# Mixture-of-experts tiles of 256 rows, with one small tile of 128 rows for each expert's odd block

## The reference, cut to what matters

```python
logits = xt @ Wr + br                       # 6250 x 8
top_p, top_idx = top_k(softmax(logits), 2)
weights = top_p / top_p.sum(-1)
xn = layernorm(xt)
xe = xn * ln_g[e] + ln_b[e]                 # per expert e
h = gelu(xe @ W1[e] + b1[e])                # 256 -> 1024
y = h @ W2[e] + b2[e]                       # 1024 -> 256
out = sum over the two chosen e of weights * y
```

## Time and profile before

| | us |
|---|---|
| median of 3 runs | 1971.73 (1967.81 to 1977.33) |
| the profiled execution | 1971.06 |
| its span on the core | 1969.4 |
| PE / DVE / ACT / POOL busy in the span | 1594.7 / 1144.1 / 884.5 / 1136.7 |

### The profile page before, as it was taken

One profiled execution on the slowest core, in us unless ns is written; L12 is line 12 of the kernel. 1 busy time (PEld: TensorE's weight loads), 2 busy tenths in 40 slices (PEclk: granted clock), 3 DMA queues, 4 the chain that ended last, 5 costly groups with the idle time before them and its releaser, 6 DMA issues. The chain is left out here.

```text
span 1969.4 us, 32441 instructions
## 1 busy us (share of the span) xinstructions
PE 1594.7 (81%) x8582; PEld 1313.8 (67%) x8583; DVE 1144.1 (58%) x3175; ACT 884.5 (45%) x1872; POOL 1136.7 (58%) x1141
## 2 busy tenths in 40 slices
PE   6766667767777787887777836789999999999997
PEld 5645455555655554555555635679999999999996
DVE  6622222322345466675765679767777777777774
ACT  6611111111213233343443456556666666666664
POOL 3177777777777677777777627753333333333333
PEclk9988888888888899998888955689999999999999
DMA  8344444344346667666677557598778887877875
GB/s 217 116 128 127 110 121 121 115 119 119 112 137 227 203 191 223 205 209 206 211 225 222 144 183 259 175 301 233 222 219 216 217 220 223 219 215 214 217 222 127
DMA packets 188121, 368.81 MB, mean 187 GB/s; under 512 B 33324, under 2 KB 134172, under 8 KB 173656
## 3 DMA queue, kind: packets, MB, share of 16 engines
q0 software_dynamic: 77296, 252.50, 45.5%
q1 hardware_dynamic: 102992, 113.64, 18.2%
q10 hardware_dynamic: 7736, 1.52, 0.4%
HBM read 287.94 MB, written 80.39 MB: 187 GB/s over the span
## 5 line engine op out<-in xcount | busy, mean ns | idle before, releaser
L697 POOL DMA_INDIRECT w2s_lent<-z_d,edge_tabs_lent x784 | 774.4, 988 | 293.0 <-issue 247.0
L1309 DVE TENSOR_TENSOR acc_lent<-acc_lent,bank 128x258 f32 x244 | 102.5, 420 | 473.9 <-PE bank L1818 470.5
L1818 PE MATMUL bank<-w2s_lent,G 128*128 x976 | 282.2, 441 | 110.5 <-POOLq L685 110.5
L1818 PE MATMUL bank<-w2s_lent,S_lent 128*128 x976 | 267.9, 424 | 84.2 <-POOLq L685 81.9
L2028 PE MATMUL bank<-w2s 128*128 128x512 f32 x896 | 330.6, 403 | 5.8 <-DMA w2s<-w_d 5.8
L1818 PEld LDWEIGHTS bank<-w2s_lent,G 128*128 128x128 f32 x976 | 208.6, 220 | 177.6 <-issue 141.5
L741 POOL DMA_INDIRECT out_dram<-G,acc_lent x112 | 178.7, 1596 | 211.0 <-DVE G L1652 162.5
L1818 PEld LDWEIGHTS bank<-w2s_lent,S_lent 128*128 128x128 f32 x976 | 200.1, 211 | 148.7 <-issue 115.1
L1033 ACT ACTIVATE G<-bank,acc_lent 128x256 f32<-128x256 f32 x448 | 187.9, 471 | 193.8 <-PE bank L2009 107.8
L2007 PE MATMUL bank<-w2s,acc 128*128 128x256 f32 x896 | 258.4, 288 | 3.5 <-DVE w2s L1631 3.0
L2008 PE MATMUL bank<-w2s,acc 128*128 128x256 f32 x896 | 253.3, 283 | 0.0
(11 more groups left out here) (316 smaller groups left out, 2562.8 us busy)
## 6 DMA issues: line engine op xcount, KB each, us to landing
w2s<-w_d POOLq DMA_DIRECT2D x112, 1024.0 KB, 5.7
w_d<-w2s_lent SPq DMA_DIRECT2D x64, 256.0 KB, 3.6
acc_lent<-bucket_d SPq DMA_DIRECT2D x56, 266.0 KB, 2.9
w2s_lent<-z_d,edge_tabs_lent POOLq DMA_INDIRECT x784, 2.9
bu_d<-w2s_lent SPq DMA_DIRECT2D x98, 128.0 KB, 1.8
w2s_lent<-bu_d SPq DMA_DIRECT2D x14, 768.0 KB, 8.0
w1s<-in_L_ffn_W_dram SPq DMA_DIRECT2D x8, 1024.0 KB, 6.1
w2s_lent<-in_L_ffn_W_dram SPq DMA_DIRECT2D x32, 256.0 KB, 5.2
```

The lines of the kernel that those rows point to most:

```text
L697: pool.indirect_dma_start(out=ring_rows[:, row % (RING * QUAD), 0:D], out_offset=None, in_=z_d[:, :], in_offset=bass.IndirectOffsetOnAxis( ...
L1309: dve.tensor_tensor(to, to, bank[j % DEPTH][:, 0:ACCW], ALU.add).then_inc(s["acc_done"], 1)
L1818: m = pe.matmul(bank[j % DEPTH][:, 0:ACCW], S_of[j % DEPTH][:, k, :], rows[:, ds(bases[j], ACCW)], start=(k == 0), stop=(k == QUAD - 1))
```

## The change

The number of tiles goes from 56 of 256 rows to 49 of 256 (`BIG`) and eight small ones of 128, 57 in all. `last_tiles` gives each expert floor(blocks / 2) big tiles and one small tile if its count of 128-row blocks is odd; small tiles that are left over take halves of further tiles of 256. The small tiles stand at fixed places in the order: 8, 15, 22, 29, 36, 43, 50 and the last, 56. The loop is gone: all 57 turns are written out on every engine, and waits that were computed from the loop's register are constants.

In a small tile the high and the low part of the turned rows lie side by side, in one operand of 256 columns. `layer1` then has two products where there were three: high weights x (high | low) with 256 columns, and low weights x high with 128 columns, 8 products in a quarter. The two halves of the sum stand in different columns of PSUM, so VectorE adds them (`add_terms`, new), and the Gelu reads `raw` in place of PSUM. The rest is halved in rows: transposes, `hhi`, `hlo`, `weigh`, scatter, and `layer2`, which has 2 pairs of products in a quarter in place of 4. First weights and `layer2`'s weights are loaded and split as for a big tile.

```diff
-MOE_TILES = (2 * N + EXPERTS * (MT - 1)) // MT
+UNITS = (2 * N + EXPERTS * (P - 1)) // P
+BIG = (UNITS - EXPERTS + 1) // 2
+MOE_TILES = BIG + EXPERTS
+SMALL_AT = [8 + 7 * k for k in range(EXPERTS - 1)] + [MOE_TILES - 1]
...
-            repeat(eng, links, two, EARLY // 2 - 1, MOE_TILES // 2 - 1)
-            body(MOE_TILES - 2, 0)
-            body(MOE_TILES - 1, 1)
+        def moe_tiles(eng, body):
+
+            for i in range(2, MOE_TILES):
+                if i == EARLY - 2:
+                    eng.wait_ge(s["moetab_set"], 2)
+                body(i, i % 2)
...
+            def add_terms(t, q):
+
+                dve.wait_ge(s["h_mm"], MOE_PARTS * t + q + 1)
+                until(dve, s["h_hi"], MOE_PARTS * t + q - 1)
+                until(dve, s["h_split"], MOE_PARTS * t + q - 1)
+                two = bank[q % 2][:, :].rearrange("p (k n) -> p k n", n=MT)
+                L.after(dve.tensor_copy(hidden_raw(t, q), two[:, :, P:2 * P]))
+                dve.tensor_tensor(hidden_raw(t, q), two[:, :, 0:P], hidden_raw(t, q), ALU.add).then_inc(s["h_sum"], 1)
...
+                if in_range(i, 1) and small(i + 1):
+                    add_terms(i + 1, 0)
                 for q in range(MOE_PARTS):
                     if in_range(i, 2):
                         first_weights(i + 2, q, e)
                     if in_range(i, 1):
+                        if small(i + 1) and q + 1 < MOE_PARTS:
+                            add_terms(i + 1, q + 1)
                         dve.wait_ge(s["h_hi"], MOE_PARTS * (i + 1) + q + 1)
...
-                        act.wait_ge(s["h_mm"], n + 1)
-                        until(act, s["h_split"], n - 1)
+                        if small(i + 1):
+                            act.wait_ge(s["h_sum"], sums_done(i + 1, q))
+                            frm, w = raw[q % 2], P
+                        else:
+                            act.wait_ge(s["h_mm"], n + 1)
+                            until(act, s["h_split"], n - 1)
+                            frm, w = bank[q % 2], MT
...
+                        if small(t):
+                            x_both = xhi[par][:, k * MT:(k + 1) * MT].bitcast(F32R)
+                            pe.matmul(to, hi, x_both, start=(k == 0), stop=(k == DC - 1), skip_group_check=True)
+                            m = pe.matmul(to[:, 0:P], lo, x_both[:, 0:P], start=False, stop=(k == DC - 1), skip_group_check=True)
+                            continue
```

More of the change, by code:

```diff
@@ L328, in build_program @@
         early_rows = tiny2(2)
+        less_half, at_slot, small_no = (tiny2(1) for _ in range(3))
         small3 = [xTs[:, :], edge_tabs[:, RT * PAYW:2 * P * EJ]]
@@ L397, in build_program, with small, halves, slot_of @@
         out_t = out.rearrange("(t p) d -> p t d", p=P)
[L399 to L406, removed]
-            repeat(eng, links, two, EARLY // 2 - 1, MOE_TILES // 2 - 1)
-            body(MOE_TILES - 2, 0)
-            body(MOE_TILES - 1, 1)
+        def moe_tiles(eng, body):
[3 more added lines that the diff above has]
+                body(i, i % 2)
+        def small(t):
+            return t in SMALL_AT
+        def halves(t):
+            return 1 if small(t) else 2
+        def slot_of(t):
+            if small(t):
+                return SMALL_SLOT + SMALL_AT.index(t)
+            return t - sum(at < t for at in SMALL_AT)
+        def added(t):
+            return 16 * sum(halves(k) for k in range(t))
+        def sums_done(t, q):
+            return MOE_PARTS * SMALL_AT.index(t) + q + 1
         def turns_of_a(t):
@@ L591, in _, with load_xe @@
                     load_ub(g + 2)
-            def load_xe(t, h, turn):
-                r = sp.value_load(moetab[0:1, ds(t, 1)], min_val=0, max_val=PADROW)
+            def load_xe(t):
+                h, n = t % 2, halves(t)
+                r = sp.value_load(moetab[0:1, slot_of(t):slot_of(t) + 1], min_val=0, max_val=PADROW)
                 until(sp, s["xe_free"], t - 1)
[L596 to L600, removed]
+                sp.dma_start(xe[h][:, 0:n, :], bucket_d[ds(r, n * P), :].rearrange("(j p) w -> p j w", p=P)).then_inc(pair["xe_in"][h], 16)
             sp.wait_ge(s["moetab_set"], 1)
@@ L1598, in last_tiles @@
             def last_tiles():
-                rc, ec = ss6[:, 0:1], ss6[:, 1:2]
+                rc, ec, rc_odd, ec_odd, is_odd, at = (ss6[:, k:k + 1] for k in range(6))
                 dve.wait_ge(s["mtab_cnt"], 2)
@@ new lines, in last_tiles @@
+                L.after(dve.tensor_scalar(ci, ci, 7, None, ALU.logical_shift_right))
+                dve.tensor_copy(units, ci)
+                L.after(dve.tensor_scalar(row8.bitcast(I32), ci, 1, None, ALU.logical_shift_right))
+                L.after(dve.tensor_copy(ntf, row8.bitcast(I32)))
+                dve.scalar_tensor_tensor(out=row8, in0=ntf, scalar=float(MT), in1=eoff, op0=ALU.mult, op1=ALU.add)
+                L.after(dve.scalar_tensor_tensor(out=odd, in0=ntf, scalar=-2.0, in1=units, op0=ALU.mult, op1=ALU.add))
@@ L1614, in last_set @@
+                dve.tensor_tensor(rc_odd, rc_odd, rc, ALU.subtract)
+                L.after(dve.tensor_tensor(ec_odd, ec_odd, ec, ALU.subtract))
+                dve.scalar_tensor_tensor(out=tile_table[:, 0:1], in0=rc_odd, scalar=is_odd, in1=rc, op0=ALU.mult, op1=ALU.add)
+                dve.scalar_tensor_tensor(out=tile_table[:, 1:2], in0=ec_odd, scalar=is_odd, in1=ec, op0=ALU.mult, op1=ALU.add
+                                         ).then_inc(s["mtab_ready"], 1)
             def last_set():
@@ L2040, in moe @@
                     if q == 1 and in_range(i, 2):
[L2041 to L2053 removed]
+                        turn_x(i + 2, par, (i + 2) // 2)
             layer1(0, 0, 0)
@@ L2064, in _ @@
             moe(1, 1)
-            for turn in range(1, EARLY // 2 - 1):
-                two(turn)
-            pe.wait_ge(s["moetab_set"], 2)
-            repeat(pe, None, two, EARLY // 2 - 1, MOE_TILES // 2 - 1)
-            moe(MOE_TILES - 2, 0)
-            moe(MOE_TILES - 1, 1)
+            moe_tiles(pe, moe)
 N_WEIGHTS = 20
```

157 lines of the change are left out of this document (89 added, 68 removed).

## The result

| | before | after |
|---|---|---|
| median, us | 1971.63 (1967.81 to 1977.33, 4 runs) | 1981.93 (1977.95 to 1985.81, 4 runs) |
| ratio | | 1.0059 (95% interval 1.0041 to 1.0077) |
| the profiled execution, its span | 1971.06, 1969.4 | 1977.95, 1976.3 |
| expert stage: start of the transposes of tile 3 to the end of the span | 1307.78 to 1969.4: 661.6 | 1304.46 to 1976.3: 671.8 |

The changed kernel is 0.6% slower. The last line of the table leaves out what varies between executions ahead of the experts (in this one the profile of after reached tile 3 earlier by 3.3 us), so the traces are compared by it: **+10.2 us**.

The account below looks back on a forecast made before the run. TensorE was taken to bound the expert stage at 12.04 us a turn. Seven big tiles less (-84.3), seven inner small ones (+84.4) and the last (+8.4) gave +8.5 on 1971.06, 1979.6, forecast as 1980 us; range 1966 to 1998.

Parts of the forecast that it names:

- TensorE alone: TensorE's own work for a small tile, layers 1 and 2, transposes and bias: 6.5 us, bounds 6.0 and 9.8.
- The chain sets the turns: Around a small tile, serial sum, Gelu and first weights on VectorE and ScalarE, 2.83 us a quarter, set two turns.
- turns s-1 and s: Turn s-1 does layer 1 of small tile s, turn s its layer 2; turn s begins at 13.24, s+1 at 24.27.
- Wait before quarter 2: In turn s-1, TensorE idles 2.1 us before quarter 2 of layer 1, needing the hhi of quarter 0.
- Its links: Per quarter: copy and add 0.89 us, two Gelus with handover 0.56, first weights' high part 0.63, handover 0.14, low part 0.61.
- An inner small tile costs 12.05 us: Each of seven small tiles before the last costs as much as a big one; halved matmuls are paid back as waiting.
- removing the branch gives nothing: Writing out the expert loop gains zero, since transposes stand 12.04 us apart also across the loop's end.
- The last tile saves 3.6 us: Tile 56, without successor, has a short VectorE chain and costs 12.04 - 3.6 us; bounds of the saving 2.8 and 5.5.
- Rival 1, the clock: Clock falls in TensorE's new waits around small tiles: +5 to +21 us on top, 1985 to 2000; chance 0.22.
- Rival 2, TensorE the bound: TensorE still sets the turns, sums and Gelus running ahead of first weights: 1936 to 1965, mostly 1939; chance 0.07.
- Rival 3, a lighter chain: Small tiles' chain lighter than its bounds, or last tile and missing loop give more: about 1965 us; chance 0.06.
- Rival 4, fetches: Written-out turns starve for instructions beside weight loads, some 40 more packets for TensorE: 2015 if each costs 1 us; chance 0.05.

Follow-up runs that it names:

- the written-out run: The kernel before, still with 56 tiles of 256 rows, with only the loops over the tiles written out: 1967.93 us, ratio 0.9990 to before.
- the run with the sums ahead: The changed kernel with copy and sum of quarter q+1 put ahead of the first weights' low part of quarter q on VectorE: 1966.82 us, ratio 0.9984 to before.

## Why the prediction was right, and where it wasn't

Forecast 1980 (1966 to 1998), measured 1981.93. The total is close, and partly by luck: two terms of the sum were off, by -2.7 and +4.2 us, and their errors nearly cancel:

| term, us | predicted | measured |
|---|---|---|
| one turn more | 12.04 | 12.04 |
| seven inner small tiles against big ones | +0.1 | -2.6 |
| small last tile | -3.6 | -3.5 |
| the end of the program | 0 | +4.2 (drain 3.8) |
| sum | +8.5 | +10.2 |

The -2.6 is the distance from the transposes of tile 3 to those of tile 56, 53 turns: 635.5 us after, 53 x 12.04 = 638.1 before. The two rows below it split one difference, the 0.7 us by which after's stretch from the last transposes to the end is longer than before's, by means of the run with a big last tile.

- **TensorE alone, 6.5 us** (6.0 to 9.8): measured 6.8 without the sums. Two products, 256 and 128 columns, take 0.23 us together where I had 0.12 + 0.09 = 0.21. The step holds.
- **The chain sets the turns.** Right, and shown by three runs from different sides: taking the sums out frees TensorE, a link more lengthens the turn by its full length, and the same links in another order shorten it. Predicted turns s-1 and s of 13.24 and 11.03 us, measured 13.40 and 10.28 at s = 15, where the clock fell in turn s-1, and 13.1 and 10.6 at s = 22 and 36, where it stayed at 1.00; the pair takes 23.7 us either way, where 24.27 was predicted. Wait before quarter 2 predicted 2.1, measured 1.68 us.
- **Its links.** Copy 0.42 (0.43 predicted), sum 0.42, first weights' high part 0.61 (0.63); the two Gelus give way to the next instruction after 0.60 (0.53). A quarter takes 2.87 to 2.94 us, 2.83 predicted. From the formulas on the page VectorE: DVE Perf Modes of the Trainium skill (section on the TRN2 errata) one works out, as an estimate, 424 ns for the sum, which the trace agrees with (0.42 us), and 392 ns for the copy, where the trace has 0.42 us and decides.
- **An inner small tile costs 12.05 us.** Mis-sized: 11.5 at four of the seven, 11.9 at the three with VectorE's further gap, 11.7 in the mean. At s = 15, from the start of turn s-1 to the next weighing I had 17.25 us; it is 1471.47 - 1454.69 = 16.78. Of the 0.47, 0.20 is the way from the weighing to the first quarter, 2.79 us where I took 2.99 and wrote that nothing there changes; 0.09 is a weighing that begins earlier, at 1.67; the rest, 0.18, lies between the first sum and the next weighing, where quarters 0 and 1 are 0.15 longer than predicted and what follows them 0.33 shorter. Turn s has the shorter way once more (1471.47 to 1474.26, again 2.79). So the step that failed is **"removing the branch gives nothing"**: for the kernel before that is true, as the written-out run shows, but the table read that it shortens lay under TensorE there, and in a small tile it lies in the chain, twice, 0.4 of the 0.55 us.
- **The last tile saves 3.6 us.** Right, 3.5 us by the run with a big last tile. The trace of after alone had misled me on it.
- **The end** had no term. I followed the work up to the last scatter and not what comes after it; the earlier trace rows show a scatter, not the drain.
- **Rival 1, the clock.** Its condition came true: at three of seven small tiles the clock fell to 0.50, the level of 1.2 GHz, for 3.4 us, as in the earlier trace rows, behind 1.68 to 2.03 us of idle. Its price, put at 0 to 1 us for one stretch in turn s-1, was nothing, since the chain covers it. It is real as soon as the cover is thinner: about 0.8 us a fall in the run with the sums ahead. Why it falls at some small tiles and stays at others, with the same wait ahead, is open.
- **Rival 2, TensorE the bound**, needed sums that don't hold up the chain. That is what the run without them is, at 1946; I had 1939 for that case.
- **Rival 3, a lighter chain**, is half true: lighter by 0.4 us a tile in the mean, not by the 2 us that 1965 would have taken.
- **Rival 4, fetches**: the written-out loop alone costs nothing. Whether the three gaps of 0.35 us on VectorE are fetches, no run shows.

## What to carry to other kernels

Halving a tile took TensorE's work from 12.04 to 6.8 us, but the instructions that the other engines issue for it do not get half as long (a pair of Gelus 0.60 us in place of 0.72), and one link added to a path that goes back and forth between two engines counts in full, with the waiting at both ends: here two instructions of 0.42 us in each of four quarters cost 4.7 us. If TensorE can take the extra work (one more product added up in PSUM), let it have it rather than an engine in the chain; if not, put the new link where it runs beside the other engine's part. And price a freed bit of time by where it will lie after the change: what slack hid before may be on the path then.

## What the runs showed of the hardware

- A float32r product of 128 columns stands 0.11 us from the next one in a stream of its like, hardly less than one of 256 columns (0.12); next to one of 256 columns the pair takes 0.23 us, of which the short one's start stands 0.06 ahead of the next.
- Reading a table entry at a fixed place left VectorE a gap 0.18 us shorter than at a place from a register (0.57 us with the loop written out, 0.75 in the loop).
- GpSimd's drain behind its last scatter ended 3.65 and 3.7 us after the scatter's issue in the two kernels without small tiles and 7.1 to 7.5 us after it in nine kernels with them; it lasted the same 9.191 or 9.192 us in seven of the nine. The scatter itself landed as fast in before and after; the cause is open.
- The granted clock fell to 0.50 for 3.4 us behind 1.7 to 2.0 us of idle, at three of seven places that look alike; where another engine's chain set the turn, the fall cost nothing.
